# Attention stage: unrolled query blocks, a maximum over 32 queries by 160 keys, and four identity products of TensorE per block

## What is computed

```python
qkv = x @ Wqkv + bqkv                      # 16 heads of 8 channels
scores = einsum('bhid,bhjd->bhij', q, k) * 8 ** -0.5
band = abs(idx[:, None] - idx[None, :]) <= 64
attn = softmax(where(band, scores, finfo.min), axis=-1)
out = einsum('bhij,bhjd->bhid', attn, v)   # heads joined again
return out @ Wout + bout
```

## Time and profile before

| | us |
|---|---|
| median of 3 runs | 856.33 |
| lowest, highest | 854.08, 858.31 |
| the profiled execution | 861.29 |
| its span, first to last instruction | 859.5 |
| attention, start to the first DMA of kmoe | 291.9 |
| of it, up to the first score product | 65.2 |

### The profile page before, as it was taken

One profiled execution on the slowest core, in us unless ns is written; L12 is line 12 of the kernel. 1 busy time (PEld: TensorE's weight loads), 2 busy tenths in 40 slices (PEclk: granted clock), 3 DMA queues, 4 the chain that ended last, 5 costly groups with the idle time before them and its releaser, 6 DMA issues. The chain is left out here.

```text
span 859.5 us, 18332 instructions
## 1 busy us (share of the span) xinstructions
PE 660.1 (77%) x7554; PEld 384.0 (45%) x7554; DVE 525.7 (61%) x1094; ACT 344.9 (40%) x522; POOL 359.2 (42%) x330
## 2 busy tenths in 40 slices
PE   0617888888888279976977498058998988999995
PEld 0302444444445179876876234023333344444442
DVE  8647667676664733342413667869999974406266
ACT  1421433444344573242414552346544536434320
POOL 9202444444444300000001253228999974966530
PEclk9967999999999559997977689669999999999998
DMA  3156552000000364000000640000000000000000
GB/s 76 37 107 108 89 72 32 0 0 0 0 0 2 111 199 100 3 4 2 4 4 5 261 112 0 0 1 0 0 1 0 0 1 1 1 0 1 12 13 25
DMA packets 17327, 29.76 MB, mean 35 GB/s; under 512 B 3248, under 2 KB 13168, under 8 KB 16240
## 3 DMA queue, kind: packets, MB, share of 16 engines
q1 hardware_dynamic: 17264, 28.87, 14.1%
HBM read 24.54 MB, written 4.19 MB: 33 GB/s over the span
## 5 line engine op out<-in xcount | busy, mean ns | idle before, releaser
L474 ACT ACTIVATE pr_exp<-at_psum 128x1024 f32<-128x1024 f32 x68 | 69.6, 1023 | 131.9 <-PE at_psum L559 131.9
L366 DVE TENSOR_REDUCE pr_neg_max<-at_psum 128x4 f32<-128x1024 f32 x68 | 83.2, 1225 | 49.8 <-PE at_psum L541 49.8
L316 POOL TENSOR_SCALAR_AFFINE_SELECT pr_exp<-pr_exp 128x512 f32<-128x512 f32 x68 | 47.1, 692 | 159.0 <-ACT pr_exp L474 159.0
L1493 POOL TENSOR_TENSOR all_phi_b<-all_phi_b,mo_work 128x512 f32<-128x512 f32 x56 | 71.1, 1269 | 43.3 <-ACT mo_work L1699 38.6
L749 POOL TENSOR_TENSOR all_x<-all_x,ff_x_blocks 128x512 f32<-128x512 f32 x3 | 3.8, 1263 | 173.0 <-ACT ff_x_blocks L940 173.0
L1514 PE MATMUL all_psum<-all_phi,mo_xt 128*128 128x512 f32 x128 | 67.1, 651 | 7.3 <-ACT mo_work L1681 5.6
L536 PE MATMUL at_psum<-band_mask,all_ident_bf 128*128 128x512 bf16 x136 | 43.1, 400 | 38.3 <-DVE pr_q_window L359 38.3
L1463 POOL TENSOR_TENSOR mo_work<-mo_work,mo_max 128x1024 f32<-128x1024 f32 x32 | 61.3, 1916 | 22.1 <-DVE mo_max L1755 22.1
L1547 PE MATMUL all_psum<-mo_xt,all_phi_centred 128*128 128x512 f32 x128 | 65.4, 591 | 0.0
L1600 PE MATMUL all_psum<-mo_work,mo_y_slots 128*128 128x512 f32 x128 | 62.5, 595 | 1.8 <-DVE mo_work L1803 1.8
L1699 ACT ACTIVATE mo_work<-all_psum 128x512 f32<-128x512 f32 x64 | 37.7, 601 | 60.6 <-PE all_psum L1547 60.6
(11 more groups left out here) (339 smaller groups left out, 1340.2 us busy)
## 6 DMA issues: line engine op xcount, KB each, us to landing
all_expert_w<-in_expert_w SPq DMA_DIRECT2D x1, 4096.0 KB, 18.3
ff_b_up<-in_b_up SPq DMA_DIRECT2D x1, 2048.0 KB, 10.2
ff_a_up<-in_a_up SPq DMA_DIRECT2D x1, 2048.0 KB, 16.1
ff_w_down<-in_w_down SPq DMA_DIRECT2D x2, 1024.0 KB, 20.5
at_q_stack<-parts_scratch SPq DMA_DIRECT2D x24, 64.0 KB
at_k_stack<-parts_scratch SPq DMA_DIRECT2D x24, 64.0 KB
at_q_stack<-parts_scratch SPq DMA_DIRECT2D x12, 128.0 KB
at_k_stack<-parts_scratch SPq DMA_DIRECT2D x12, 128.0 KB
```

Source lines behind the costliest of these rows:

```text
L316: nc.gpsimd.affine_select(out=e[:, g, :, 0, :], in_=e[:, g, :, 0, :], compare_op=ALU.is_ge, fill=0.0, base=0, pattern=[[0, GH], [-1, P]], ...
L366: nc.vector.tensor_reduce(negm[:, GH * g:GH * g + GH].rearrange("p (u r) -> p r u", r=2), psum[:, SN + 2 * (g % 2):SN + 2 * (g % 2) + 2, : ...
L474: nc.scalar.activation(e[:, g, :, :, :].rearrange("p h j q -> p (h j q)"), psum[:, ST:ST + 2, :].rearrange("p b n -> p (b n)"), ACT.Exp).t ...
L1493: nc.gpsimd.tensor_tensor(tot[:, ch % 2, :], first, ec[:, ch % 2, j, :], ALU.add).then_inc(added, 1)
```

## The change

`attention` is written anew; kmoe, ssm and soft_moe stay as they are. In words:

- The loop is unrolled. PE reads the stacks where they lie; the window copies of DVE (L358, L359, L362) are gone.
- SP loads x in three pieces. The parts go straight from SBUF to the stacks, without DRAM, part h as soon as it is there. Groups, sizes and destination partitions (8 per DMA) are as before. A 49th row of the stack holds the flag for keys outside the sequence. It and three rows of ones are written by six DMAs of SP before.
- The band mask is no longer a product. DVE adds it and takes the maximum in one `tensor_tensor_reduce` per head, over 160 keys: `natural` now makes four small products of 32 queries by 160 keys for each head, one per quarter of the PSUM partitions. A block has eight units of two heads.
- The maximum is not subtracted by products with a selection matrix: its three bf16 parts are copied by SP, with two DMAs for each block (`maxima_in`), into three more rows of `q_stack`, against the rows of ones in `k_stack`. `transposed` needs them, and then has four products of 128 columns per unit; ACT takes the exponential of 512 columns; three banks of PSUM rotate for it and three for `natural`. `natural` runs two blocks ahead.
- In front of every second unit of `transposed` stands one product of the identity by 512 columns, whose result is overwritten (`keep_warm`), and 24 of them stand ahead of the blocks.
- The projection and the statistics of the last norm are made tile by tile within the blocks, 12 of 16 tiles are normalised on DVE during the last two blocks, the bias is added by a product, and the constants are filled in smaller pieces.

```diff
--- before.py
+++ after.py
@@ -158,489 +158,551 @@
...
-    TERMS_Q, TERMS_K = "hhmmhl", "hmhmlh"
...
+    NU = 8
+    QC, WIN = 32, 160
+    FLAG, PARTS = 48, 49
+    WARM = 24
+    TERMS_Q, TERMS_K = "hhhmml", "hmlhmh"
+    CHUNKS = ((0, 512), (512, 1024), (1024, 1536), (1536, 2048))
+    STACKS = ((0, 512), (512, 1024), (1024, 2048))
...
+        mask = a.sb("mask", [P, WIN], BF16)
...
+                sp.wait_ge(ones_filled, 1)
+                sp.wait_ge(pads, 1)
+                sp.wait_ge(flags_filled, 1)
+                for half in range(2):
+                    p0 = 64 * half
+                    sp.dma_start(ks[p0 + FLAG:p0 + FLAG + 1, :, :], flags[:, :].unsqueeze(1).broadcast_to([1, NP, (NT + 2) * P])).then_inc(rows_in, 16)
+                    sp.dma_start(ks[p0 + PARTS:p0 + PARTS + 3, :, :], ones[:, :].unsqueeze(1).broadcast_to([3, NP, (NT + 2) * P])).then_inc(rows_in, 16)
+                    sp.dma_start(qs[p0 + FLAG:p0 + FLAG + 1, :, :], ones[0:1, 0:NW * P].unsqueeze(1).broadcast_to([1, NP, NW * P])).then_inc(rows_in, 16)
+
+                def stack(group, kind):
+                    r0, r1 = STACKS[group]
+                    sp.wait_ge({"h": hi_ready, "m": mid_ready, "l": low_ready}[kind], 2 * r1 // 512)
+                    for which, (dst, terms, pad) in enumerate(((qs, TERMS_Q, 64), (ks, TERMS_K, P))):
+                        for n, k in enumerate(terms):
+                            if k == kind:
+                                for half in range(2):
+                                    p0 = 64 * half + DH * n
+                                    sp.dma_start(dst[p0:p0 + DH, :, pad + r0:pad + r1], part[k][64 * half:64 * half + 64, which, r0:r1]).then_inc(stacked[group], 16)
+
+                def maxima_in(w):
+                    sp.wait_ge(mt_ready, w + 1)
...
+                        p0 = 64 * half + PARTS
+                        sp.dma_start(qs[p0:p0 + 3, :, w * P:w * P + P], m_t[24 * half:24 * half + 24, w % 2, :]).then_inc(nm_in[w % 2], 16)
...
-                                    p0 = 64 * half + 8 * n
-                                    sp.dma_start(stack[p0:p0 + 8, :, pad + r0:pad + r1], rows[half][:, :, r0:r1]).then_inc(stacked[ch], 16)
...
+                for kind in "hml":
+                    stack(0, kind)
+                stack(1, "h")
+                maxima_in(0)
+                stack(1, "m")
+                stack(1, "l")
+                maxima_in(1)
+                for n, kind in enumerate("hml"):
+                    stack(2, kind)
+                    maxima_in(2 + n)
+                for w in range(5, NW):
+                    maxima_in(w)
...
-                    def window(w, wp):
-
-                        dve.wait_ge(tiles_ready, w + 1)
-                        nc.vector.tensor_copy(kw[:, wp, :, :], ks[:, :, bass.ds(w * P, 2 * P)])
-                        nc.vector.tensor_copy(qw[:, wp, :, :], qs[:, :, bass.ds(w * P, P)]).then_inc(win, 1)
-
...
+                    dve.wait_ge(sn_done, n + 1)
+                    k = NU * w + m
+                    if k >= 3:
+                        dve.wait_ge(sn_free, k - 2)
+                    for i in range(2):
+                        r, j = head(m, i)
+                        last = v.tensor_tensor_reduce(out=masked[:, 2 * (k % 3) + i, :], in0=psum[:, SN + n % 3, WIN * i:WIN * i + WIN], in1=mask[:, :], scale=-1.0, scalar=3.0e38,
+                                                      op0=ALU.add, op1=ALU.min, accum_out=nm[:, r, 0, j:j + 1])
+                    last.then_inc(sn_free, 1)
...
+                def keep_warm(n, bank=5):
+
+                    for _ in range(n):
+                        nc.tensor.matmul(psum[:, bank, :].rearrange("p (k n) -> p k n", k=4), c["identb"][:, :], c["identb"][:, :].unsqueeze(1).broadcast_to([P, 4, P]), start=True, stop=True)
...
+                def natural(w, m):
+                    n = nat_unit(w, m)
+                    if m == 0:
+                        last_tile = min(w + 1, NT)
+                        for ch, (r0, r1) in enumerate(STACKS):
+                            if r0 < last_tile * P <= r1:
+                                pe.wait_ge(stacked[ch], 16 * 24)
+                    slot_free(pe, n)
+                    for i in range(2):
+                        r, j = head(m, i)
+                        rows = slice(64 * r, 64 * r + PARTS)
+                        for q in range(0, P, QC):
+                            k0 = w * P + q
+                            last = nc.tensor.matmul(psum[q:q + QC, SN + n % 3, WIN * i:WIN * i + WIN], qs[rows, j, k0:k0 + QC], ks[rows, j, k0:k0 + WIN], start=True, stop=True)
+                    last.then_inc(sn_done, 1)
+
+                def transposed(w, m):
+                    n = NU * w + m
+                    if m == 0:
+                        pe.wait_ge(nm_in[w % 2], 32 * (w // 2 + 1))
+                    if n >= 3:
+                        pe.wait_ge(exp_done, n - 2)
+                    if m % 2 == 0:
+                        keep_warm(1, ST + n % 3)
+                    for i in range(2):
+                        r, j = head(m, i)
+                        rows = slice(64 * r, 64 * r + PARTS + 3)
+                        for b in range(2):
+                            last = nc.tensor.matmul(psum[:, ST + n % 3, 256 * i + P * b:256 * i + P * b + P], ks[rows, j, (w + b) * P:(w + b) * P + P], qs[rows, j, w * P:w * P + P], start=True, stop=True)
+                    last.then_inc(st_done, 1)
...
+                keep_warm(WARM)
...
+                for w in range(2):
+                    for m in range(NU):
+                        natural(w, m)
+                    maxima_t(w)
+                for s in range(NW):
+                    for m in range(NU):
+                        transposed(s, m)
+                        if s + 2 < NW:
+                            natural(s + 2, m)
+                        if m == 0 and s >= 1:
+                            values(s - 1, 2)
+                        if m == 1 and s >= 1 and s + 1 < NW:
+                            maxima_t(s + 1)
+                        if m == 1 and s >= 3:
+                            project(s - 3)
+                        if m == 2 and s >= 1:
+                            values(s - 1, 3)
+                        if m == 4 and s >= 1:
                             values_nat(s - 1)
...
```

799 lines of the change are left out of this document (385 added, 414 removed).

## The result

The changed kernel takes 911.85 us (median of four, 908.18 to 912.37) where the kernel before, beside it on the same chip, takes 857.32 (854.08 to 859.47): a ratio of 1.063, with a 95% interval of 1.0585 to 1.0676. The forecast was 823, the range ended at 850. It is rival D: TensorE works through the whole loop at half its clock. The profiled execution took 912.1, its span is 910.3.

The account below looks back on a forecast made before the run. PE was taken to bound the blocks, a transfer the prologue. Start 38, maxima 14.4, blocks of 10.9, waits and epilogue 12.0 put kmoe at 258.6, was 291.9: 861.3 less 33.3 is 828.0, median 823, range 795 to 850.

Parts of the forecast that it names:

- rival D: Attention loop: products in parts of the array drop PE to 1.2 GHz, block 18.2 us, total 927; chance 0.11.
- the block of 10.9 us: Attention loop: one block at 2.4 GHz takes 10.9 us, was 12.0, bounds 10.2 and 12, with PE the limit.
- half clock after gaps: Loop: after each DMA wait PE resumes at half clock, costing 2 us in sum.
- First `natural` at 38: Prologue: first score product starts at 38 us, was 65.2, set by 24 stack DMAs taking 21.3 us.
- Two blocks of maxima in 14.4: Ahead of the loop: two `natural` blocks alone take 14.4 us, DVE the limit at 0.37 us a head.
- DMA waits of 8.9 and 4.8: Loop: blocks 2 and 3 wait 8.9 and 4.8 us for maxima queued behind the stack DMAs.
- Blocks: Attention loop: blocks of 10.9 us, the last two, without `natural`, 8.0 and 7.0 up to the last unit.
- Epilogue of 12.0: End of attention, up to kmoe's first DMA: shrinks from 18.4 to 12.0 us.
- The rest: Everything from kmoe's first DMA on: taken as unchanged at 567.6 us.
- C: Maxima on DVE: 0.65 us a head makes DVE the bound, block 12.3 us, block 0 at 61.2, total 837; chance 0.10.
- B: Prologue transfers: twice the rate, first `natural` at 33, no DMA waits, 802 us, or 791 with shorter blocks; chance 0.15.

Follow-up runs that it names:

- one burst: Changed kernel plus 24 more identity products of 512 columns in one go ahead of block 4: 838.3 us (before 862.0).
- the products moved: Changed kernel with the last stack DMAs issued in six pieces and the 24 identity products placed behind the maxima, directly ahead of block 0: 904.4 us.
- the burst in the wait: Changed kernel plus 24 identity products ahead of the wait for the DMA of block 2: 905.6 us.
- bursts ahead of 0 and 1: Changed kernel, last stack DMAs in six pieces, 24 identity products ahead of blocks 0 and 1 each: 810.7 to 821.1 us in four executions, 898.6 profiled.
- split stacks: Changed kernel with the last 24 stack DMAs issued in six pieces, the maxima of blocks 2 to 6 going out between them: 904.1 us.
- bursts ahead of four blocks: Changed kernel, last stack DMAs in six pieces, 24 identity products ahead of each of blocks 0 to 3: 821.0 us (before 861.8).
- pairs of row halves: Changed kernel with two units issued alternately, product by product, each on its half of the array's rows: 813.0 us; with further edits 791.9 to 803.0.

## Why the prediction was wrong

The step that failed is the price of the loop's columns at 2.4 GHz, the block of 10.9 us, which took 16.44, and with it the chance of 0.11 for D. Against D I had put the four identity products, "0.85 us of full array in each block", without a row that showed that they are enough. The runs show that four a block kept the clock for 129 us behind one burst, where without them it was gone after 17; that they did not always keep it (it fell in block 0 with the products moved, in block 2 with the burst in the wait, in block 3 with bursts ahead of 0 and 1); and that they brought it back in no execution. With eight a block it came back only in block 15. What I had not thought of is that the loop can run at either clock for as long as it lasts, with the same instructions, and that it would enter block 0 at the lower one. I took 2 us for "half clock after gaps", as in the kernel before, whose loop wins the clock back by itself; the changed one does not.

I had also misread. The stretch of kmoe at 1.00 has no larger tiles than the one at 0.56, where they are 64*64 and 64*32: they are all 64*64, with 128 columns to a product; PE was busy 9.80 of its 10 us, against 8.83. This is its only group of products, from 410 to 420 us in the kernel before:

```profile
L1061 PE MATMUL ff_psum<-ff_one_hot_t,ff_b_up 64*64 64x128 f32 x312 | 10.3, 276 | 0.2 <-issue 0.2
```

So tiles of a quarter of the array can run at 1.00, and the size of a tile alone does not set the clock. At 32 ns from one to the next (312 in 10 us), where 128 columns take 53 at 2.4 GHz, more than one of them ran at a time.

In the terms of the sum, on the profiled execution (828.0 forecast, 912.1 measured, 84.1 apart):

- First `natural` at 38: 42.62. The transfer was right: where the 24 products stood elsewhere, the stacks were there at 37.9 to 41.4. I had laid the products under the transfer; they began at 35.64, ran 7.04 us (5.35 in other runs, by the clock) and set the start.
- Two blocks of maxima in 14.4: 10.5 us. The reduce is 0.25 us a head, not 0.37. Both errors cancel: `transposed` 0 came at 53.15 for 52.4. So 0.8 us.
- DMA waits of 8.9 and 4.8: 7.9 and none. The transfers ran at 70 GB/s in 60 to 80 us, as assumed; block 3 came too late to wait. With the 2 us for the clock that is 7.8 us less.
- Blocks: from block 0 to the last unit 178.5 us without waits forecast, 264.9 measured (325.96 - 53.15 - 7.9): 86.4 us more. At 10.26 us a block, as with the burst, it would have been less than forecast. D had 18.2 us for a block at half clock and so 927; it was 16.44. I had doubled 7.3 us of columns; the blocks of 10.26 and 16.44 differ by 6.2.
- Epilogue of 12.0: 14.5. At half clock, and POOL's select took 2.92 us instead of 0.63 beside DVE's twelve additions, so the last `values` waited 1.3 us.
- The rest 2.3 us longer. Sum: 0.8 - 7.8 + 86.4 + 2.5 + 2.3 = 84.2.

The mark I gave for D was met: the clock was under 0.71 from 120 to 230 us. C's mark (`transposed` 0 at 61) was not, nor B's. The warning on gaps that I quoted is only half of it. Rows first: the clock fell in a wait of 1.57 us and 1.8 us behind one of 1.3, but also 3.4 us behind 24 full products with no wait at all, and in the kernel after it stayed at 0.50 from 88 to 326 us, with a PE that was never idle. By the rule in the Trainium skill, "TensorE: Matmul & The Clock Gate", section "Why this matters for your kernels", which asks for a TensorE kept busy and without idle gaps, closing the gaps would have brought the clock back; closing them (split stacks) gave 904.1 us at 0.50.

What stays open: why the clock falls in one block and not in the next. It fell in block 0 in the profiled execution with bursts ahead of 0 and 1, and held there with bursts ahead of four blocks, though up to block 2 both run the same instructions. Most runs here are one execution of a loop that can do either, so a clock that held or fell in one of them may do the other in the next; the kernels with several executions are the changed one (four, all low), the one with bursts ahead of 0 and 1, and the three with pairs of row halves (four, four and six, all under 800 us). Nor is it shown what in the small products matters, the rows that they fill or the changes of shape between them. In the last two blocks, without `natural`, the clock came back with no identity product (at 287.6 and 297.8) and with eight, and not with four.

## What to carry to other kernels

When a change replaces full-array products by products in parts of the array, price the loop at both clocks and give the lower one a large chance, also where no wait is added; look for a stretch of the same shapes in the same trace and take its clock. A loop can run at either clock for its whole length: a few full products may keep a clock that they do not bring back, so look at the clock at which it is entered, and time several executions. Filling the idle half of the array with a second unit is worth more than filler products: it cut columns and changes of shape (9.0 for 10.3 us a block), and with it the clock came back by itself.

## What the runs showed of the chip

- With the same instructions a block took 10.26 us at a clock of 1.00 and 16.44 at 0.50, and with four identity products a block the lower clock, with no burst behind, lasted to the end of the loop in every profiled execution in which it was there.
- The part of the array that products fill bears on the clock: the same columns and count at 128 rows instead of 52 took 820.8 us (one execution), not 911.9, with no burst; four changes of shape a block fell away with it.
- With the same instructions up to block 2 the clock fell in block 0 in one execution and held there in another; one program took 898.6 us in one execution and 810.7 to 821.1 in four.
- A change of tile shape costs 0.11 us at 1.2 GHz and 0.10 at 2.4: it is not a matter of columns.
- The reduce over 160 elements from PSUM, with its accumulator read (0.08), runs every 0.25 us on DVE.
- POOL's select over 512 elements took 2.92 us instead of 0.63 while DVE added twelve tiles in SBUF.
- DMAs from SBUF to 8 partitions of SBUF ran at 70 GB/s with a DMA share of 0.55, as those from DRAM had the earlier trace rows; a small DMA issued by ScalarE landed 14 us after its issue (69.05 to 82.92) while they ran.
